# Operands of split attention loaded in two sets of 72 partitions, from parts stored three times

## The reference

```
Q = split(q_in @ wq + bq, Sq)          # 16 heads of 8 channels
K = split(k_in @ wk + bk, Sk)          # Sk = 512 (context) or 256 (self)
scores = einsum('bhqd,bhkd->bhqk', Q, K) / HD ** 0.5
probs = softmax(scores, axis=-1)
ctx = einsum('bhqk,bhkd->bhqd', probs, V)
```

## Time and profile before

| what | us |
|---|---|
| median of 3 runs | 1580.05 |
| lowest and highest run | 1578.64, 1587.03 |
| the profiled execution's own time | 1580.41 |
| its span in the profile | 1578.6 |
| PE busy in the span | 1310.2 (83%) |
| DVE, ACT, POOL busy | 921.2, 678.8, 317.3 |

### The profile page before, as it was taken

The page is one execution under the profiler, slowest core; times in us unless marked ns, Lnnn a source line. Parts: engine busy times, 40 slices in busy tenths (PEclk is TensorE's granted clock), DMA queues, the critical chain, the costliest instruction groups (busy, mean ns, idle before and its releaser), DMA issues.

```text
span 1578.6 us, 27744 instructions
## 1 busy us (share of the span) xinstructions
PE 1310.2 (83%) x8424; PEld 645.0 (41%) x8424; DVE 921.2 (58%) x1954; ACT 678.8 (43%) x1017; POOL 317.3 (20%) x891
## 2 busy tenths in 40 slices
PE   1699999899999976878759999995538989868998
PEld 0244445434444433444314444442215656533333
DVE  4488888443444433666536888873545767534544
ACT  1276776533333323665516766672202444412221
POOL 5332231100000003332132332211222333100000
PEclk9999999989999996998958999998757999969999
DMA  4443434100000003333243333312213333101000
GB/s 133 122 133 110 121 107 151 62 20 7 27 7 27 15 28 112 102 103 113 93 128 91 109 111 118 104 35 77 73 51 99 90 92 90 53 24 40 27 21 14
DMA packets 123904, 119.99 MB, mean 76 GB/s; under 512 B 16128, under 2 KB 97800, under 8 KB 123792
## 3 DMA queue, kind: packets, MB, share of 16 engines
q1 hardware_dynamic: 123792, 118.62, 25.4%
HBM read 78.98 MB, written 38.80 MB: 75 GB/s over the span
## 4 chain that ended last, share of the span: by engine, by line
issue 46%; PE 29%; POOLq 10%; DVE 6%; DMA 4%; SPq 3%; ACT 1%; DVEq 1%; ACTq 0%; POOL 0%; PEldq 0%
PE s_ps L1278 5%; PE e_ps L1317 5%; PE av_ps L1335 4%; PE e_ps L1442 3%; PE e_ps L1443 2%; PE av_ps L1466 2%; DMA Qst<-mrow 2%; DVE nmax L1002 2%; PE s_ps L1285 2%; POOLq L785 1%; POOLq L766 1%; PE misc L1346 1%; POOLq L827 1%; POOLq L769 1%; SPq L687 1%
## 5 line engine op out<-in xcount | busy, mean ns | idle before, releaser
L862 ACT ACTIVATE prob<-e_ps 128x1024 f32<-128x1024 f32 (+1 forms) x384 | 379.6, 989 | 241.0 <-PE e_ps L1317 184.3
L1002 DVE TENSOR_REDUCE nmax<-s_ps 128x1 f32<-128x512 f32 x512 | 340.4, 689 | 85.0 <-PE s_ps L1278 81.2
L1317 PE MATMUL e_ps<-Qst,Kst 99*128 99x256 bf16 x1408 | 238.0, 282 | 42.2 <-DMA Qst<-mrow 42.0
L1335 PE MATMUL av_ps<-prob,Vx 128*32 128x256 f32 (+1 forms) x3072 | 243.8, 386 | 2.6 <-ACT OT L865 2.5
L1006 DVE TENSOR_REDUCE nmax<-s_ps 128x2 f32<-128x512 f32 x256 | 173.7, 689 | 113.0 <-PE s_ps L1285 61.1
L1278 PE MATMUL s_ps<-Kst,Qst 72*128 72x512 bf16 x512 | 207.6, 409 | 26.1 <-DVE nmax L1002 20.7
L1466 PE MATMUL av_ps<-prob,wbig 128*128 128x512 f32 x384 | 191.5, 597 | 0.0
L1317 PEld LDWEIGHTS e_ps<-Qst,Kst 99*128 99x128 bf16 x1408 | 134.3, 100 | 108.4 <-DMA Qst<-mrow 34.7
L1185 DVE TENSOR_TENSOR prob<-prob,s_ps 128x512 f32<-128x512 f32 x128 | 87.8, 687 | 148.0 <-ACT prob L935 146.9
L1453 PE MATMUL e_ps<-fin,wbig 128*128 128x512 f32 x288 | 158.8, 650 | 1.1 <-DMA fin<-feat_ffn 1.1
L935 ACT ACTIVATE prob<-e_ps,b 128x512 f32<-128x512 f32 x128 | 88.0, 687 | 153.2 <-PE e_ps L1453 153.2
(11 more groups left out here) (155 smaller groups left out, 1619.8 us busy)
## 6 DMA issues: line engine op xcount, KB each, us to landing
Qst<-q_parts SPq DMA_DIRECT2D x384, 48.0 KB
Kst<-k_parts SPq DMA_DIRECT2D x192, 96.0 KB
Kst<-k_parts SPq DMA_DIRECT2D x192, 48.0 KB
q_parts<-qp SPq DMA_DIRECT2D x32, 192.0 KB, 2.1
k_parts<-kp SPq DMA_DIRECT2D x16, 384.0 KB, 2.6
inT<-feat_att SPq DMA_DIRECT2D x32, 128.0 KB, 2.8
ctxT<-in_ctxT SPq DMA_DIRECT2D x16, 256.0 KB, 3.0
k_parts<-kp SPq DMA_DIRECT2D x16, 256.0 KB, 2.9
```

The costliest lines, as they stand in the source:

```text
L862: act.activation(dst, src, ACT.Exp).then_inc(probs_ready, 1)
L1002: ve.tensor_reduce(nmax[:, g, u, h % GH:h % GH + 1], s_ps[:, u, :], AX.X, ALU.max, negate=True).then_inc(s_drained, 1)
L1317: last = pe.matmul(o, Ks[0:KROWS, par, h, t * P:t * P + P], Qst[0:KROWS, par, h, :], start=True, stop=not a.rope)
L1335: last = pe.matmul(av_ps[VW * hh:VW * hh + VW, SQ - w:SQ], Vx[:, par, t, h, :], prob[:, slot % RING, off * SQ:off * SQ + w], start=(t == 0 ...
```

## The change

Q's parts are stored as (part, copy), each part three times, by three DMAs with a repeated source; K's parts as (copy, part), by three DMAs. The scratch then has the nine pairs in the order of the partitions, so that one transfer of 72 partitions brings Q and one brings K, for eight heads at a time (`HALVES = 2`), at places 0 and 4. The K store of 512 keys moves from place 14 to 10 and that of 256 keys from 10 to 9; the second K split moves from 9 to 6. Semaphore counts follow.

```diff
-PARTS_AT, RES_AT, INPUTS_AT = (0, 3, 7, 11), 4, 12
-HALVES = 4
+PARTS_AT, RES_AT, INPUTS_AT = (0, 4), 4, 12
+HALVES = 2
...
             if a.kt > 2:
-                put(9, ("ksplit", b + 2, 1, 0))
-            put(10 if a.kt == 2 else 14, ("kstore", b + 2, None, 0))
+                put(6, ("ksplit", b + 2, 1, 0))
+            put(9 if a.kt == 2 else 10, ("kstore", b + 2, None, 0))
...
-        q_scr = scratch("q_parts", (2, PARTS, P, SQ), BF16)
-        k_scr = scratch("k_parts", (2, (2 * PARTS - 1) * P * SC), BF16)
+        q_scr = scratch("q_parts", (2, PARTS * PARTS, P, SQ), BF16)
+        k_scr = scratch("k_parts", (2, PARTS * PARTS * P * SC), BF16)
...
-                    sp.dma_start(q_scr[par].rearrange("t p c -> p t c"), qp[:, :, :]).then_inc(q_stored[par], 16)
+                    dst = q_scr[par].rearrange("(t r) p c -> p t r c", r=PARTS)
+                    for t in range(PARTS):
+                        src = qp[:, t, :].unsqueeze(1).to_broadcast([P, PARTS, SQ])
+                        sp.dma_start(dst[:, t, :, :], src).then_inc(q_stored[par], 16)
                 elif kind == "kstore":
                     sp.wait_ge(k_split, (n + 1).on(j))
-                    dst = k_parts(par, a.keys).rearrange("t p c -> p t c")
-                    sp.dma_start(dst[:, 0:3, :], kp[:, :, 0:a.keys]).then_inc(k_stored[par], 16)
-                    sp.dma_start(dst[:, 3:5, :], kp[:, 0:2, 0:a.keys]).then_inc(k_stored[par], 16)
+                    dst = k_parts(par, a.keys).rearrange("(r t) p c -> p r t c", r=PARTS)
+                    for r in range(PARTS):
+                        sp.dma_start(dst[:, r, :, :], kp[:, :, 0:a.keys]).then_inc(k_stored[par], 16)
...
-                    for r in range(PARTS):
-                        sp.dma_start(Qst[w * r:w * r + w, par, hs, :], q_src[:, hs, :]).then_inc(qk_loaded[par][arg], 16)
+                    sp.dma_start(Qst[0:ROWS, par, hs, :], q_src[:, hs, :]).then_inc(qk_loaded[par][arg], 16)
                     sp.wait_ge(k_stored[par], stored_k)
                     k_src = k_parts(par, a.keys).rearrange("t (d h) c -> (t d) h c", h=HEADS)
-                    for r in range(PARTS):
-                        sp.dma_start(k_heads(a.keys)[w * r:w * r + w, par, hs, :], k_src[HD * r:HD * r + w, hs, :]) \
-                            .then_inc(qk_loaded[par][arg], 16)
+                    sp.dma_start(k_heads(a.keys)[0:ROWS, par, hs, :], k_src[:, hs, :]).then_inc(qk_loaded[par][arg], 16)
```

More of the change, by code:

```diff
@@ L263, in program @@
         rows["x"], rows["out"] = dram["x"], outs[0]
-        q_scr = scratch("q_parts", (2, PARTS, P, SQ), BF16)
-        k_scr = scratch("k_parts", (2, (2 * PARTS - 1) * P * SC), BF16)
+        q_scr = scratch("q_parts", (2, PARTS * PARTS, P, SQ), BF16)
+        k_scr = scratch("k_parts", (2, PARTS * PARTS * P * SC), BF16)
         def k_parts(par, keys):
-            rows = k_scr[par][0:(2 * PARTS - 1) * P * keys]
-            return rows.rearrange("(t p c) -> t p c", t=2 * PARTS - 1, p=P)
+            rows = k_scr[par][0:PARTS * PARTS * P * keys]
+            return rows.rearrange("(t p c) -> t p c", t=PARTS * PARTS, p=P)
         RES = {"att0": ("x", "x1"), "att1": ("z", "y1"), "att2": ("y1", "y2"), "att3": ("z4", "u")}
@@ L653, in att_step @@
                 elif kind == "qstore":
-                    before = early(n.half() * 96, j, 0)
+                    before = early(n.half() * 32, j, 0)
                     sp.wait_ge(q_split, (n + 1).on(j))
@@ L659, in att_step @@
                             sp.wait_ge(qk_loaded[par][hf], before)
-                    sp.dma_start(q_scr[par].rearrange("t p c -> p t c"), qp[:, :, :]).then_inc(q_stored[par], 16)
+                    dst = q_scr[par].rearrange("(t r) p c -> p t r c", r=PARTS)
+                    for t in range(PARTS):
+                        src = qp[:, t, :].unsqueeze(1).to_broadcast([P, PARTS, SQ])
+                        sp.dma_start(dst[:, t, :, :], src).then_inc(q_stored[par], 16)
                 elif kind == "kstore":
                     sp.wait_ge(k_split, (n + 1).on(j))
-                    dst = k_parts(par, a.keys).rearrange("t p c -> p t c")
-                    sp.dma_start(dst[:, 0:3, :], kp[:, :, 0:a.keys]).then_inc(k_stored[par], 16)
-                    sp.dma_start(dst[:, 3:5, :], kp[:, 0:2, 0:a.keys]).then_inc(k_stored[par], 16)
+                    dst = k_parts(par, a.keys).rearrange("(r t) p c -> p r t c", r=PARTS)
+                    for r in range(PARTS):
+                        sp.dma_start(dst[:, r, :, :], kp[:, :, 0:a.keys]).then_inc(k_stored[par], 16)
                 elif kind == "loadqk":
-                    stored_q = early((n.half() + 1) * 16, j, 0)
-                    stored_k = early((n.half() + 1) * 32, j, 1)
+                    stored_q = early((n.half() + 1) * 48, j, 0)
+                    stored_k = early((n.half() + 1) * 48, j, 1)
                     done = (arg + 1) * a.slots // HALVES
@@ L678, in att_step @@
                     hs = slice(HH * arg, HH * arg + HH)
-                    w = PARTS * HD
                     sp.wait_ge(q_stored[par], stored_q)
                     q_src = q_scr[par].rearrange("t (d h) c -> (t d) h c", h=HEADS)
-                    for r in range(PARTS):
-                        sp.dma_start(Qst[w * r:w * r + w, par, hs, :], q_src[:, hs, :]).then_inc(qk_loaded[par][arg], 16)
+                    sp.dma_start(Qst[0:ROWS, par, hs, :], q_src[:, hs, :]).then_inc(qk_loaded[par][arg], 16)
                     sp.wait_ge(k_stored[par], stored_k)
                     k_src = k_parts(par, a.keys).rearrange("t (d h) c -> (t d) h c", h=HEADS)
-                    for r in range(PARTS):
-                        sp.dma_start(k_heads(a.keys)[w * r:w * r + w, par, hs, :], k_src[HD * r:HD * r + w, hs, :]) \
-                            .then_inc(qk_loaded[par][arg], 16)
+                    sp.dma_start(k_heads(a.keys)[0:ROWS, par, hs, :], k_src[:, hs, :]).then_inc(qk_loaded[par][arg], 16)
                 elif kind == "maxT":
@@ L868, in att_step @@
                     if n.m or n.k >= 1:
-                        act.wait_ge(q_stored[1 - par], ((n + 1).half() * 16).on(j))
+                        act.wait_ge(q_stored[1 - par], ((n + 1).half() * 48).on(j))
                     c = CI[a.name + "_q"]
@@ L879, in att_step @@
                     if n.m or n.k >= 1:
-                        act.wait_ge(k_stored[1 - par], ((n + 1).half() * 32).on(j))
+                        act.wait_ge(k_stored[1 - par], ((n + 1).half() * 48).on(j))
                     c = CI[a.name + "_k"]
@@ L1013, in att_step @@
                     ve.wait_ge(misc_filled, (m + 1).on(j))
-                    stored, per = (q_stored, 16) if kind == "q" else (k_stored, 32)
+                    stored, per = (q_stored, 48) if kind == "q" else (k_stored, 48)
                     ve.wait_ge(stored[1 - par], ((n + 1).half() * per).on(j))
@@ L1272, in att_step @@
                     if u == 0 and s % (a.slots // HALVES) == 0:
-                        pe.wait_ge(qk_loaded[par][s // (a.slots // HALVES)], ((n.half() + 1) * 96).on(j))
+                        pe.wait_ge(qk_loaded[par][s // (a.slots // HALVES)], ((n.half() + 1) * 32).on(j))
                     Ks = k_heads(a.keys)
```

## The result

The changed kernel takes **1626.12 us** (median of 4 runs, 1622.89 to 1628.63), the kernel before 1582.37 in the same session (4 runs, 1578.64 to 1587.03): a ratio of 1.028, interval 1.025 to 1.0311. It is 44 us slower. The forecast was 1573.2 us, range 1559 to 1586: wrong side, and outside the range. Rival C (slower, because the load ahead of a rows transfer is slow) is what happened, at a larger size than its 1599 us.

A forecast was written before the change was run, and what follows sets the result against it. PE bounds att0; in the 256-key layers PE mainly waits for `Qst<-mrow` rows blocked behind SyncE's issues. Terms -9.1 + 4.2 - 2.1 = -7.0 us on 1580.41 gave 1573.4, stated as 1573.2 us; range 1559 to 1586.

The forecast's parts named there:

- Rival C: Rival: slower, as 72-row loads move no faster than earlier bursts, 175 GB/s, and rows land late; 1599 us, chance 0.10.
- SyncE as what blocks the rows: Att1 and att3: rows transfers queue behind other DMAs SyncE issues, 0.4 us each; 7 us per batch of issuing saved.
- groups after the K store: Four att1 batches: rows go out when ACT has them, 2.5 us; weights issued earlier, 0.5 us; together 3.0 us gained.
- Groups after the output stores: Nine groups in att1 and att3: rows issued and landing earlier; gain 10.0 us, at most 11.9, at least nothing.
- L+2.95: Groups after the output stores: predicted landing of the rows, 2.95 us after L, the issue of the first load.
- Steady 512-key batches: zero: Att0 and att2: no change, since rows behind 864 KB land at L+3.7 and E started at L+5.36.
- Clock: One drop to half clock gone in layers with waits: -2.1 us; bounds 0 and four gone, 8.4.
- Stage starts: Start of each attention stage: extra K data delays the first S matmul; sum +4.2 us, bounds 0 and +8.
- hold-up of att3 (-1.2): Att3's start: three K issues took 2.37 us, half of it a hold-up that att1 and att0 lack; counted -1.2 us.
- Stores: Stores rise from 3 to 6 per batch; extra K data priced at stage starts, 1.5 us (512 keys), 0.8 (256).
- Rival C's sum: 1580 + 11 (steady att0 and att2 batches) + 9.8 (stage starts) - 2.1 (3.0 x 0.7 won) = 1599 us; chance 0.10.
- Its threshold, 227 GB/s: Rival C decides once 864 KB ahead of the rows need over 3.9 us, 227 GB/s; chance 0.10.

The follow-up runs named there:

- experiment 9: Changed kernel with the same 72 rows at other partitions (0 to 31, 64 to 95, every fourth of 32 to 60), in three transfers: ratio 1.0258.
- experiment 5: Changed kernel with each 72-partition load cut into one of 64 partitions and one of 8: ratio 1.0421.
- experiment 1: Changed kernel with four sets of four heads at places 0, 3, 7, 11 in place of two of eight, 72-partition loads kept: 0.9923, 1570.31 us.
- experiment 4: Kernel before with two sets of eight heads at places 0 and 4, its stores and 24-partition loads kept: ratio 1.0411.
- experiment 8: Changed kernel with each load of eight heads cut into two of four heads, same bytes and places: ratio 1.0264.
- Experiment 3: Changed kernel with threefold stores kept, but four sets at 0, 3, 7, 11 loaded 24 partitions at a time: ratio 1.0133, 1596.57 us.
- experiment 6: Changed kernel with four sets of four heads at places 1, 6, 10, 14, each just behind a rows transfer: ratio 1.0062.

## Why the prediction was wrong, by its own steps

**SyncE as what blocks the rows: right.** In att1 the rows now go out 0.88 us after the first load (702.61 to 703.49) where it was 2.50. In the groups after the K store, where the earlier trace rows show waits of 0.88 to 0.38 us in four batches, only the first still waits (0.83 us): most of that term came in. The waits for rows in att1's steady part other than those of the next step fell from 12.7 to 6.5 us.

**The step that failed** is the one under "Groups after the output stores" that costs the load ahead of the rows: "590 kB / 396 = 1.5 us", rows at L+2.95, with 396 GB/s from a weight load. The loads move at about half of that. In att2 a whole set takes 4.3 us at 204 GB/s (2 us in the midst of it reach 233). In att1, with the rows 0.88 us behind the load, E starts at L+5.15 (707.76) and not at L+2.95, and five such groups wait 2.99 to 3.71 us each where four had waited 1.76 to 3.20 (the first of them is in the earlier trace rows). So the gain of 10.0 us became a loss. The group (timeline of the kernel after), and behind it PE's waits in att1:

```profile
702.61 0.34 SPq L684 DMA_DIRECT2D Qst<-q_parts  x1
...
703.49 0.79 SPq L691 DMA_DIRECT2D Qst<-mrow  x1
...
707.76 0.61 PE L1316 MATMUL e_ps<-Qst,Kst 99*128 99x256 bf16 x4 [3.06 <-DMA Qst<-mrow]
```

```profile
PE e_ps L1316 <- DMA Qst<-mrow: 25.0, 18, 3.7
```

25.0 us, where the earlier trace rows have 24.2 and the forecast saw the two layers fall from 36 to some 20. The weight load (396 GB/s over 0.9 us) goes to all 128 partitions, an operand load (204) to the first 72. Whether that is what makes the difference is not shown: rows at other partitions move no faster (experiment 9, 228 against 233 GB/s over 2 us). A higher busy share of the DMA engines, 0.87 in place of 0.74, brings only 223 GB/s in place of 204 (experiment 5).

**"Steady 512-key batches: zero" failed with it.** 864 KB at 396 GB/s put the rows at L+3.7; they come at L+6.45, 1.1 us later than E used to start, exactly as rival C had it (L+6.5, 1.1 us). Experiments 1, 4 and 8 show that the volume ahead of the rows is the cause of the loss: half the volume removes it (0.9923), the large set alone brings it on in the kernel before (1.0411), and cutting the same volume finer changes nothing (1.0264).

**Clock: wrong sign.** One drop less (-2.1 us) was forecast, with up to four as bound; in fact +22.0 us, the largest single term. The prediction counted drops in the layers with waits alone and none for att0 and att2, and rival C priced a wait of 1.1 us at 1.1 us (times 0.7), where one of 2.62 us was followed by 6.5 us at half clock, 3.3 us more of work time. In att0 there was none before: its clock was 1.00. But only about 30 of the 50 us more at half clock lie at waits for rows, and of att0's 17 us only 7; the other 10 follow a wait that the kernel before has at full clock. So a longer wait can have this second price and often has it here; no run shows when.

**Stage starts: sign right, size half.** +4.2 us was forecast, bounds 0 and +8; ahead of the four stages 4.8 + 1.8 + 3.1 + 0.2 = 9.9 us came. In att0 (chain, start us, us):

```profile
50.37 4.09 DMA k_parts<-kp
...
54.48 6.81 DMA Kst<-k_parts
```

The store lands in 4.09 us instead of 2.94, +1.2 us where +1.5 was forecast. The K load takes 6.81 us where the chain of the kernel before has 2.78, +4.0 against a forecast of +0.5. From 54.5 to 61.3 the core's DMAs move 196 GB/s, in 6.8 us some 1.33 MB, over twice the K load's own 590 kB: the rate is again half of what was forecast, and what is issued ahead of the load and right behind it moves at the same time. With four sets the K load takes 3.74 us and with eight 2.62. The hold-up of att3 (-1.2) may be gone; its start is the one that hardly grew.

**Stores: under-costed outside the starts.** Experiment 3 finds +1.3% (0.7 to 1.96) for the threefold stores, against almost nothing in the forecast, which priced only those at the start of a stage. Which traffic they meet was not tried.

**Rival C's sum** fell short by 27 us on the time (1599 against 1626.12), of which the session's slower kernel before is 2, and by 24 on the spans (18.7 against 42.5): its +11 for the steady batches of att0 and att2 was 27.7 in truth (14.4 + 13.3), 15.7 of it clock, and att1 and att3, for which it had -2.1, added 6.7; its +9.8 for the starts came to 9.9; 1.8 came back behind att3. Its threshold, 227 GB/s, lay above the 204 measured, and it had the right row for it, 175 GB/s; a chance of 0.10 was too low for it. That today's bursts had not filled the queues was taken to mean that larger transfers would go far faster; the rate rose from 175 to 204.

## What to carry to other kernels

Before a transfer is made larger, ask which small, urgent transfer stands behind it: what that one paid here was about the whole large one's data time (4.34 us from issue to E behind a set that moves in 4.30), at the rate of a transfer of the same kind (204 GB/s), not that of whatever filled the queues (396). Cut the number of issues and the bytes ahead separately: one wide transfer in place of three was worth 26 us here, and doubling the set cost more than that, so the wide transfer with the old set size beats both kernels (1570.31 us). Moving loads behind the urgent transfer only helps while they still reach their own reader in time (experiment 6: S waits 24.4 us for its K load, 5.4 in experiment 1). Price a wait in a stretch where TensorE is the bound as a range: its own length, or that and what its clock does afterwards (2.62 us and, in one case here, 3.3 more).

## What was not expected of the hardware

- The urgent transfer on another engine's queue is not faster but slower: 5.42 us from issue to use against 4.34 with the loads ahead of it on the same queue, and the kernel goes from 1.028 to 1.0786. The runs don't show whether the loads issued ahead of the rows or those issued just behind them hold them there. At 1.0786 the time also has PE's longer stretches at half clock in it.
- Loads of 72 rows moved at 204 to 233 GB/s however they were cut or placed (windows of 2 to 4.3 us; shares 0.74, 0.87, 0.86), weight loads to 128 partitions at 396 in a window of 0.9 us. Whether the number of partitions or the reads of the scratch in HBM hold the rate was not tried.
- PE's busy time is no constant of the work: 8424 matmuls took 1310.2 us before and 1328.4 after, and a wait of 1.48 us was followed by full clock in one kernel and by 10 us at half clock in the other.
